# Scores of an attention's first unit moved into the stage ahead, and five loops over sequences written out

## The reference, cut to what matters

```python
q = layernorm((x @ Wq.T).heads(16)); k = layernorm((x @ Wk.T).heads(16)); v = (x @ Wv.T).heads(16)
x = causal_softmax(q @ k.T) @ v @ Wo.T + bo                    # first attention, head width 16
h = layernorm-like(x)                                          # the residual of the block
q = rope((h @ Wq2).heads(16)); ckv = h @ Wkva                  # head width 64
k = [ckv[:R] @ Wkvb, rope(ckv[R:])]; v = ckv[:R] @ Wkvb
x = h + causal_softmax(q @ k.T / 8) @ v @ Wo2                  # second attention
out = x + shared(rmsnorm(x)) + sum_e comb_e * (silu(x Wg_e) * (x Wu_e)) @ Wd_e
```

## Time and profile before

| | us |
|---|---|
| median of 3 runs (3895.45 to 3899.51) | 3897.67 |
| the profiled execution | 3898.49 |
| its span | 3896.6 |
| PE busy | 3423.8 (88%), 31584 matmuls |
| PEld busy | 2711.6 (70%) |
| DVE busy | 2787.2 (72%) |
| ACT busy | 2418.9 (62%) |
| POOL busy | 1084.6 (28%) |
| mean granted clock of TensorE | 0.953 of full speed |
| instructions executed | 92993 |
| packets of instruction queues q8 and q14 | 285 of 4.67 MB, 247 of 2.02 MB |

### The profile page before, as it was taken

One profiled execution on the slowest core, in us unless ns is written; L12 is line 12 of the kernel. 1 busy time (PEld: TensorE's weight loads), 2 busy tenths in 40 slices (PEclk: granted clock), 3 DMA queues, 4 the chain that ended last, 5 costly groups with the idle time before them and its releaser, 6 DMA issues.

```text
span 3896.6 us, 92993 instructions
## 1 busy us (share of the span) xinstructions
PE 3423.8 (88%) x31584; PEld 2711.6 (70%) x31584; DVE 2787.2 (72%) x5934; ACT 2418.9 (62%) x6426; POOL 1084.6 (28%) x762
## 2 busy tenths in 40 slices
PE   3688898988989889898988989889898888989988
PEld 2477676776767767676776767767677776767767
DVE  3676777767777776777767767777777767777775
ACT  2656666665666756667566666656667565676664
POOL 1324231242412324222242412324122242312420
PEclk9799999999999999999999999999999999999999
DMA  3000000000000000000000000000000000000000
GB/s 76 1 7 7 7 2 11 3 7 7 2 13 2 7 7 6 9 2 8 7 7 7 2 13 2 7 7 2 13 2 7 7 7 7 2 8 7 7 1 7
DMA packets 33908, 30.36 MB, mean 8 GB/s; under 512 B 8865, under 2 KB 33313, under 8 KB 33377
## 3 DMA queue, kind: packets, MB, share of 16 engines
q1 hardware_dynamic: 33376, 23.68, 2.1%
HBM read 15.28 MB, written 8.39 MB: 6 GB/s over the span
## 4 chain that ended last, share of the span: by engine, by line
PE 67%; ACT 11%; issue 9%; DVE 6%; POOL 6%; SPq 1%; ACTq 0%; DMA 0%; DVEq 0%; POOLq 0%
PE bank L664 14%; PE scores L766 9%; PE bank L675 7%; ACT prob L926 7%; PE scores L651 6%; PE scores L652 5%; PE bank L790 4%; PE scores L720 4%; PE scores L653 3%; PE bank L635 3%; PE bank L611 2%; POOL qf L527 2%; PE scores L647 2%; PE scores L740 2%; ACT qkt L872 2%
## 5 line engine op out<-in xcount | busy, mean ns | idle before, releaser
L926 ACT ACTIVATE prob<-scores,negmax 128x128 f32<-128x128 f32 (+3 forms) x2048 | 1060.0, 536 | 283.1 <-DVE negmax L1155 237.7
L1155 DVE TENSOR_REDUCE negmax<-scores 128x1 f32<-128x128 f32 (+3 forms) x2048 | 885.7, 484 | 144.9 <-PE scores L653 86.0
L664 PE MATMUL bank<-ident,prob 128*128 128x128 f32 x5120 | 747.7, 284 | 48.7 <-DVE probt L1163 39.4
L1163 DVE COPY probt<-bank 128x512 f32<-128x512 f32 x896 | 597.8, 685 | 198.8 <-PE bank L664 192.2
L664 PEld LDWEIGHTS bank<-ident,prob 128*128 128x128 f32 x5120 | 562.5, 145 | 163.3 <-DVE probt L1163 70.1
L653 PE MATMUL scores<-mask,ident 128*128 128x128 bf16 x2048 | 462.2, 237 | 0.0
L651 PE MATMUL scores<-khh,qt 128*128 128x256 f32 (+2 forms) x1024 | 442.1, 432 | 22.4 <-issue 21.6
L926 ACT ACTIVATION_READ_ACCUMULATOR prob<-scores,negmax 128x1 f32 x2048 | 434.7, 212 | 0.0
L486 POOL TENSOR_TENSOR otl<-onm,oth 128x512 fp32r<-128x512 f32 x96 | 122.7, 1278 | 897.0 <-ACT oth L872 897.0
L497 POOL TENSOR_TENSOR rq<-ssq,expo 128x32 f32<-128x32 f32 x64 | 359.9, 5630 | 39.6 <-DVE ssq L1126 39.6
L481 POOL COPY rexp<-rsum 128x512 f32<-128x512 f32 x128 | 78.1, 610 | 1045.6 <-DVE rsum L1167 1045.6
(11 more groups left out here) (184 smaller groups left out, 6669.6 us busy)
## 6 DMA issues: line engine op xcount, KB each, us to landing
x_in<-in_x_rows SPq DMA_DIRECT2D x16, 512.0 KB, 3.5
out_rows<-x SPq DMA_DIRECT2D x16, 512.0 KB, 4.6
r_gu<-in_wg SPq DMA_DIRECT2D x2, 512.0 KB, 4.9
r_gu<-in_wu SPq DMA_DIRECT2D x2, 512.0 KB, 5.6
r_d<-in_wd SPq DMA_DIRECT2D x1, 1024.0 KB, 6.9
r_wqt<-in_wq_nope_t SPq DMA_DIRECT2D x1, 512.0 KB, 6.6
r_wqr<-in_wq SPq DMA_DIRECT2D x2, 256.0 KB, 8.5
r_wob<-in_wo SPq DMA_DIRECT2D x1, 512.0 KB, 5.1
```

What stands on the lines that cost most here:

```text
L664: ins = nc.tensor.transpose(bank[4 + n % 2][:, q * P:(q + 1) * P], prob[:, u % 2, q, i * P:(i + 1) * P], ident[:, :])
L926: nc.scalar.activation(prob[:, u % 2, q, 0:n], bank[q][:, 0:n], ACT.Exp, bias=negmax[:, a, u, q:q + 1], accum_out=sums[:, a, u, q:q + 1]). ...
L1155: nc.vector.tensor_reduce(negmax[:, a, u, M * part:M * part + M], scores[:, M * part:M * part + M, 0:n], axis=AX.X, op=ALU.max, negate=Tru ...
L1163: nc.vector.tensor_copy(probt[:, u % 2, i], bank[4 + n % 2][:, :]).then_inc(probt_dve.sem, 1)
```

## The change

All five loops over sequences are written out in Python, so that every threshold is a constant and no engine jumps.

Unit 0 of both attentions leaves `attend` (except attention 0 of the first sequence). For attention 0 of sequence b + 1, TensorE issues the scores in e = NE, after the last quads and ahead of the last down product; VectorE takes the maxima ahead of the last addition; ScalarE computes the exponentials at the end of the experts, and loads the table of exp directly behind the last silu instead of at the end. For attention 1, TensorE issues the scores ahead of the last two `transpose_q`; ScalarE and VectorE do their part in step n = 2 NT. The waits that stood ahead of the scores of unit 0 (the last `qt` copies, `vb`, all quads) now stand behind the scores of unit 1, ahead of the first transposes.

On the side of the key, `khh` moves from step 5 to step 4, and the two parts of `kll` from steps 6 and 7 to steps 5 and 6. The statistics of the next input (`first_stats`) move from steps 8 and 9 to steps 3 to 6, one tile each, and the variance to step 7.

```diff
--- before.py
+++ after.py
@@ -444,7 +444,7 @@
 
         sp.wait_ge(weights_ready, len(SPLIT))
         sp.dma_start(x_in[:, :, :], dram["x"][0].rearrange("(t p) c -> p t c", p=P)).then_inc(x_loaded.sem, 16)
-        with sp.Fori(0, NB - 1) as b:
+        for b in range(NB - 1):
             sp.wait_ge(y_added.sem, y_added.at(b, NT))
             sp.dma_start(x_in[:, :, :], dram["x_rows"][bass.ds(b * L + L, L)].rearrange("(t p) c -> p t c", p=P)).then_inc(x_loaded.sem, 16)
             sp.wait_ge(down_added.sem, down_added.at(b, 1))
@@ -527,7 +527,7 @@
                 nc.gpsimd.tensor_tensor(qf[:, n % 2, :, R:DK], ta[:, n % 2], tb[:, n % 2], ALU.add).then_inc(rope_ready.sem, 1)
 
 
-                if n - KV_STEP in (1, 2, 3, 6, 7):
+                if n - KV_STEP in (1, 2, 3, 5, 6):
                     pool.wait_ge(rope_ready.sem, rope_ready.at(b, n + 1))
                 if n == KV_STEP + 1:
                     pool.wait_ge(kv_copied.sem, kv_copied.at(b, 1))
@@ -537,10 +537,10 @@
                 if n == KV_STEP + 3:
                     nc.gpsimd.tensor_tensor(kf[R:2 * R], ka[R:2 * R], kb[R:2 * R], ALU.add).then_inc(kf_ready.sem, 1)
                     pool.wait_ge(kf_ready.sem, kf_ready.at(b, 1))
-                if n == KV_STEP + 6:
+                if n == KV_STEP + 5:
                     pool.wait_ge(khh_ready.sem, khh_ready.at(b, 1))
                     chain.link(nc.gpsimd.tensor_tensor(kll[0:DK], kf[0:DK], khh[0:DK].bitcast(F32), ALU.subtract))
-                if n == KV_STEP + 7:
+                if n == KV_STEP + 6:
                     nc.gpsimd.tensor_tensor(kll[DK:2 * DK], kf[0:DK], khh[0:DK].bitcast(F32), ALU.subtract).then_inc(kll_ready.sem, 1)
                     pool.wait_ge(kll_ready.sem, kll_ready.at(b, 1))
             if not last:
@@ -551,7 +551,7 @@
                 prepare(b + 1)
             chain.end(last)
 
-        with pool.Fori(0, NB - 1) as b:
+        for b in range(NB - 1):
             sequence(b, last=False)
         sequence(NB - 1, last=True)
 
@@ -685,14 +685,21 @@
             ins.then_inc(rsumt_psum.sem, 1)
 
         def attend(b, a, last):
-            for part in range(NM):
-                score(b, a, 0, part)
-            if a == 0:
-                pe.wait_ge(down_added.sem, down_added.at(b, 0))
+            if a == 0 and b == 0:
+                for part in range(NM):
+                    score(b, a, 0, part)
             for u in range(UNITS):
                 if u + 1 < UNITS:
                     for part in range(NM):
                         score(b, a, u + 1, part)
+                if u == 0:
+                    if a == 0:
+                        pe.wait_ge(down_added.sem, down_added.at(b, 0))
+                        pe.wait_ge(stackt_act.sem, stackt_act.at(b, 4 * NT))
+                    else:
+                        pe.wait_ge(qt_act.sem, qt_act.at(b, 2 * NT))
+                        pe.wait_ge(qt_dve.sem, qt_dve.at(b, 2 * NT))
+                        pe.wait_ge(vb_ready.sem, vb_ready.at(b, 1))
                 early = EARLY[tile_of(u)]
                 transpose_prob(b, a, u, range(early))
                 if u > 0:
@@ -792,7 +799,8 @@
             ins.then_inc(down_psum.sem, 1)
 
         def sequence(b, last):
-            pe.wait_ge(stackt_act.sem, stackt_act.at(b, 4 * NT))
+            if b == 0:
+                pe.wait_ge(stackt_act.sem, stackt_act.at(b, 4 * NT))
             attend(b, 0, last)
 
             transpose_tokens(b, 1)
@@ -809,12 +817,13 @@
                     for t in range(NT):
                         ins = nc.tensor.transpose(bank[6][:, t * R:(t + 1) * R], kf[0:R, t * P:(t + 1) * P], ident[0:R, 0:R])
                     ins.then_inc(vb_psum.sem, 1)
+            pe.wait_ge(kll_ready.sem, kll_ready.at(b, 1))
+            pe.wait_ge(nope_ready.sem, nope_ready.at(b, 2 * NT))
+            pe.wait_ge(rot_ready.sem, rot_ready.at(b, 2 * NT))
+            for part in range(NM):
+                score(b, 1, 0, part)
             transpose_q(b, 2 * NT - 2)
             transpose_q(b, 2 * NT - 1)
-            pe.wait_ge(qt_act.sem, qt_act.at(b, 2 * NT))
-            pe.wait_ge(qt_dve.sem, qt_dve.at(b, 2 * NT))
-            pe.wait_ge(kll_ready.sem, kll_ready.at(b, 1))
-            pe.wait_ge(vb_ready.sem, vb_ready.at(b, 1))
             attend(b, 1, last)
 
             if not last:
@@ -848,6 +857,10 @@
                     spread_comb(b, e)
                 if e + 1 < NE:
                     gate_up(b, e + 1)
+                if e == NE and not last:
+                    pe.wait_ge(hid_ready.sem, hid_ready.at(b, NE))
+                    for part in range(NM):
+                        score(b + 1, 0, 0, part)
                 if e == 0:
                     transpose_comb(b)
                 else:
@@ -860,7 +873,7 @@
         for n in range(4 * NT):
             transpose_quad(0, n)
 
-        with pe.Fori(0, NB - 1) as b:
+        for b in range(NB - 1):
             sequence(b, last=False)
         sequence(NB - 1, last=True)
 
@@ -946,14 +959,15 @@
         def attend(b, a):
             for u in range(UNITS + 1):
                 mine = []
-                if u < UNITS:
+                here = u > 0 or a == 0 and b == 0
+                if u < UNITS and here:
                     for part in range(NM // 2):
                         exps(b, a, u, part)
                 if u % NT == 1 and u > NT:
                     copy_out(b, a, u // NT - 1)
                 if 0 < u <= UNITS:
                     mine = [i for i in range(tile_of(u - 1) + 1) if acts(first_block(u - 1) + i)]
-                if u < UNITS:
+                if u < UNITS and here:
                     for part in range(NM // 2, NM):
                         exps(b, a, u, part)
                 for i in mine:
@@ -985,14 +999,17 @@
                     if n >= 3:
                         act.wait_ge(qt_psum.sem, qt_psum.at(b, 2 * (n - 2)))
                     copy(stq[:, (n - 1) % 2, :, 0], qf[:, (n - 1) % 2]).then_inc(qh_ready.sem, 1)
+                if n == 2 * NT:
+                    for part in range(NM):
+                        exps(b, 1, 0, part)
                 if n == KV_STEP:
                     act.wait_ge(kv_psum.sem, kv_psum.at(b, 1))
                     copy(kf[0:3 * R], bank[6][0:3 * R]).then_inc(kv_copied.sem, 1)
-                if n == KV_STEP + 5:
+                if n == KV_STEP + 4:
                     act.wait_ge(kf_ready.sem, kf_ready.at(b, 1))
                     copy(khh[0:DK], kf[0:DK])
                     copy(khh[DK:2 * DK], kf[0:DK]).then_inc(khh_ready.sem, 1)
-                if n == KV_STEP + 4:
+                if n == KV_STEP + 5:
                     act.wait_ge(vb_psum.sem, vb_psum.at(b, 1))
                     copy(vb[:, :, :], bank[6][:, 0:NT * R].rearrange("p (t r) -> p t r", t=NT)).then_inc(vb_ready.sem, 1)
             attend(b, 1)
@@ -1016,6 +1033,8 @@
                     if e >= 2:
                         act.wait_ge(hidl_ready.sem, hidl_ready.at(b, e - 1))
                     nc.scalar.activation(sg[:, e % 2], bank[2 * (e % 2)][:, :], ACT.Silu).then_inc(silu_ready.sem, 1)
+                    if e == NE - 1:
+                        act.preload_act_table_set("natural_log_exp_and_others")
                 if e > 0:
                     act.wait_ge(hid_ready.sem, hid_ready.at(b, e))
                     if e >= 3:
@@ -1031,7 +1050,9 @@
                 if e == 0:
                     act.wait_ge(combt_psum.sem, combt_psum.at(b, 1))
                     copy(combt[0:3 * E], bank[5].bitcast(BF16)[0:3 * E, 0:L]).then_inc(combt_ready.sem, 1)
-            act.preload_act_table_set("natural_log_exp_and_others")
+            if not last:
+                for part in range(NM):
+                    exps(b + 1, 0, 0, part)
 
         act.wait_ge(padded, 3)
         split_first(0)
@@ -1045,7 +1066,7 @@
             if t + 2 < NT:
                 cast_parts(0, t + 2)
 
-        with act.Fori(0, NB - 1) as b:
+        for b in range(NB - 1):
             sequence(b, last=False)
         sequence(NB - 1, last=True)
 
@@ -1175,7 +1196,7 @@
 
         def attend(b, a, last):
             for u in range(UNITS + 1):
-                if u < UNITS:
+                if u < UNITS and (u > 0 or a == 0 and b == 0):
                     for part in range(NM):
                         maxima(b, a, u, part)
                 mine = []
@@ -1257,11 +1278,13 @@
                     dve.wait_ge(qh_ready.sem, qh_ready.at(b, n))
                     s = (n - 1) % 2
                     tt(stq[:, s, :, 1], qf[:, s], stq[:, s, :, 0].bitcast(F32), ALU.subtract).then_inc(ql_ready.sem, 1)
-                if n >= 2 * NT and not last:
-                    for t in ((0, 1), (2, 3), ())[n - 2 * NT]:
-                        ins = first_stats(b + 1, t)
-            if not last:
-                first_variance(b + 1, ins)
+                if 3 <= n < 3 + NT and not last:
+                    ins = first_stats(b + 1, n - 3)
```

(10 more changed lines are left out.)

## The result

| kernel | median us | ratio to before, 95% interval |
|---|---|---|
| before, beside the changed kernel | 3898.28 | |
| the changed kernel, 4 runs (3748.66 to 3753.52) | 3750.13 | 0.9622 (0.9606 to 0.9639) |

The account below looks back on a forecast made before the run. The prediction took TensorE, two thirds of the chain of waits, as the bound, with 9% lost to "issue". Its sum was 3898.5 - 54.6 - 15 - 46 + 12 = 3794.5 us, range 3752 to 3846.

Parts of the forecast that it names:

- part D: Projection steps 3 to 6: early statistics and khh cost 0.8 us a sequence, 12 us in all.
- the other three signs: Loops written out and unit 0 moved at both attentions: each a gain, of 54.6, 15 and 46 us.
- A: Sequence boundaries: fourteen loop jumps go, each worth 3.9 us, 54.6 us gained, ends 39 and 60.
- C: Second attention's entry: unit 0 ahead of the last two q transposes gains 2.9 us a sequence, 46 us.
- B: End of the experts: the first attention's unit 0 moved there gains 1.0 us a boundary, 15 us.
- Rival 2: Both attention entries: TensorE's clock stays high, 137 us gained, 3762 us; chance 13%.
- rival 3: Exp's table load in its new place: a drain behind it adds 22 us, 3816 us; chance 4%.
- slower rival: Inside the written-out bodies: instruction fetching can't follow, stalls add 126 us, 3920 us; chance 3%.

Follow-up runs that it names:

- e5: The kernel before with loops written out and khh, kll and the next input's statistics early, both units still at the start of their attention; 3799.0 us.
- e1: The kernel before with its five loops written out and nothing else; 3826.2 us.
- e4: The changed kernel with unit 0 of attention 0 back at the start of the attention and exp's table load behind the last expert; 3769.5 us.
- e3: The changed kernel with unit 0 of attention 1 back at the start of the attention; 3783.6 us.
- e7: The changed kernel with khh back in step 5 and kll in steps 6 and 7; 3798.2 us.
- e8: e1 with twelve extra unread matmuls in each of TensorE's three idle stretches ahead of attention 1, nothing moved; 3784.5 us.
- v4: v3 with 48 extra unread matmuls on TensorE ahead of the token transposes and 12 more ahead of the tokens' hi part; 3711.2 us.
- e2: The changed kernel with sequences 1 to 14 in a loop again on all engines; 3828.3 us.
- v3: The changed kernel with ScalarE's q copy ahead of attention 1's unit 0 exponentials, and one quad each of experts 8 and 9 an expert earlier; 3745.4 us.

## Why the prediction was wrong

The step that failed is part D: a cost of 12 us was forecast, and the side moves gave 27.2 (e5 under e1), since TensorE's clock then stays up in half of the sequences. The places and the other three signs held, the sum didn't: 104 against 148. The period of a sequence fell from 235.5 to 225.5 us, where 228.5 was forecast. By the steps of the prediction, with the four parts put on one after another (e1, e5, e4, changed):

| part | forecast | measured |
|---|---|---|
| A, loops written out | 54.6 | 72.2 |
| D, side moves | -12 | 27.2 (e5 under e1) |
| C, unit 0 of attention 1 | 46 | 29.5 (e4 under e5), 33.4 with B already in (changed under e3) |
| B, unit 0 of attention 0 | 15 | 19.4 (changed under e4), 15.4 without C (e3 under e5) |

- **A** was right in its mechanism, and too small by 18 us. I read it from a single pair of boundaries. The written-out one happened to be of the slower of two kinds, 63.7 where e1's mean is 63.0: the clock goes down behind the addition in some written-out sequences and not in others, and I had read one where it does. The 0.6 us of attention 1 and the experts had no pair to read it from. The upper end that I gave, 60, was not wide enough: "waits against constants also save something elsewhere" had no price. Without loops 82394 instructions are executed instead of 92993 (e1); that this is where the 0.6 us come from wasn't tested.
- **B** was worked out step by step and came out nearly so. The last down product was to be 0.9 us late; it starts 6.98 us behind the last silu instead of 6.09, and from e4 to the changed kernel the stretch with the experts grows from 129.17 to 129.97. Unit 1's maximum was to start 1.35 us behind the addition and starts at 1.33. The gain to the variance is 63.00 - 61.30 = 1.70, where 1.0 net and 0.9 of cost make 1.9. Net that is 0.9 a boundary, 14 us; the other 5 or 6 of the 19.4 come from the projection (34.65 to 34.27), where B had forecast nothing. And a part of the 1.70 is the clock: it goes down behind the addition in seven of 15 boundaries of e4, in none of the changed kernel.
- **D** failed with its sign. I priced the four statistics and khh as VectorE's and ScalarE's work in full steps, at 0.8 us and up to 1.5. Something of it is there in the middle: the fifth of the eight groups of q transposes starts 18.71 us behind the first q product in e5 and 17.98 in e1 (sequence 2 of both). From the first group to the fifth it is 10.7 us in e5, but 9.9 in e7, which has the early statistics and the late key, as in e1. So this comes from the key and not from the statistics. At the last group it is made good (25.56 against 25.38), and unit 0 starts earlier (27.45 against 27.89). What I didn't see is that TensorE's idle time at the end of the stage gets shorter with the side moves, 3.2 us against 4.2 or 3.6, and that in half the sequences the clock then stays up (e5).
- **C** was the right place, with kll done, the q transposes behind the scores and ScalarE's queue as described (last transposes to follow the copy that follows the exponentials). I took 2.9 us, "nearer to the first" of 2.4 (clock low) and 4.0 (clock high). The clock is high over units 0 and 1 in every sequence. Together C and D were forecast as 34 us; measured are 56.7 (e4 under e1). The clock alone, with nothing moved, gave 41.7 (e8); e4, where the clock is as high at this entry, is 15.0 us faster than that.
- **Rival 2** had the mechanism, with 13%. With D at nothing instead of 12 against it, its sum would have been 3750, the measured time, but by luck: its A of 55 was 72, its B of 30 was 19, its C of 64 was 30, and D gave 27.
- **The drain behind the load** (rival 3): the load takes 1.28 us in its new place too (590.77), and the hi part starts 0.01 us after its end (592.06). The Trainium skill ("ScalarE: Activation LUTs", section What ACT_TABLE_LOAD costs) adds some 1380 ns of drain to each load; the trace doesn't agree. How much of B's 0.9 us of cost is the load's stays open: no kernel here moved it by itself.
- **The slower rival** (5, straight code that the fetching can't follow): no sign of it in e1, where the only change was the loops, nor in the changed kernel (0.03 to 0.04 us in front of each first maximum behind an addition), and the instruction queues moved less, 4.13 and 1.12 MB against 4.67 and 2.02 in the loop. (It would have taken 104 / 2.8 = 37 stalls to use up the forecast gain, not 40.)

What stays open: what decides, sequence by sequence, whether the clock goes down over unit 0 in e3 and e5, and behind the addition in e1, v4 and others. The traces show both kinds in one run, and filling the gaps is all that any experiment here did to it on purpose.

## What to carry to other kernels

Before pricing a gap on TensorE, look at the granted clock behind it: in this kernel three gaps of 1.3 to 1.4 us cost 2.6 us more in the matmuls behind them. A change that shortens such a gap can be worth more than its length, and work moved into it can be worth both. A few matmuls of no use, put in the gap, tell in one run how much. Read a loop's jump at the boundary, on the engine that has the next critical instruction, but look at several boundaries, since one pair was off by 0.8 us of 4.7.

## What the runs showed of the hardware

- A jump back in a body of this length makes VectorE stand 3.2 us in front of the next maximum in the mean of 14, 3.4 in e2 in the mean of ten. Each of the 13 jumps of e2 costs 6.0 us of time (78.2 / 13), with the clock down behind each.
- The same code in the same run has different kinds of sequences: with the clock at 2.4 or 1.2 GHz over unit 0 the projection is 35.0 or 38.4 us, 3.4 us apart (e5); with the clock up or down behind the last addition the stretch to the variance is 62.4 or 63.4 us (e1).
- A load of the table of exp took 1.28 us wherever it stood, and the next instruction of ScalarE could start 0.01 us after it (592.06).
- 60 matmuls of 128 columns in idle time of TensorE made the stretch from the variance to the transposes 2.6 us shorter a sequence (33.15 to 30.53 us, v3 to v4).
